# Leaving 246 doubly stored edges to their first place, and fetching the last group's 266 rows one by one, in a graph kernel on Trainium2

## What is computed

```python
ef = relu(edge_attr @ We1 + be1) @ We2 + be2
ef = ef * sigmoid(timestamps[:, None] @ Wt + bt)
combined = concatenate([x[src], ef], axis=1)
msg = relu(combined @ Wn1 + bn1) @ Wn2 + bn2
out = segment_sum(msg, dst, num_segments=6250) + x
result = layernorm(x + out)          # eps 1e-5, no scale or shift
```

## Time and profile before

| | |
|---|---|
| median of 3 runs | 1052.55 us (1051.5 to 1053.58) |
| profiled execution | 1052.93 us, of which the span from its first to its last instruction is 1051.1 us |
| PE busy | 851.2 us (81%) |
| DVE busy | 650.9 us (62%) |
| ACT busy | 592.4 us (56%) |
| POOL busy | 781.9 us (74%) |

### The profile page before, as it was taken

The page is one execution under the profiler, slowest core; times in us unless marked ns, Lnnn a source line. Parts: engine busy times, 40 slices in busy tenths (PEclk is TensorE's granted clock), DMA queues, the critical chain, the costliest instruction groups (busy, mean ns, idle before and its releaser), DMA issues.

```text
span 1051.1 us, 19241 instructions
## 1 busy us (share of the span) xinstructions
PE 851.2 (81%) x5031; PEld 616.9 (59%) x5032; DVE 650.9 (62%) x1688; ACT 592.4 (56%) x658; POOL 781.9 (74%) x832
## 2 busy tenths in 40 slices
PE   6899996988788788787787787887887787787884
PEld 6667674666456556465565665564564565564663
DVE  4767774766655666566466566566557566565666
ACT  5576664665465466455555555555555555555542
POOL 7777777777777777777777777777777777777773
PEclk9999999999998999889999999999999999998997
DMA  8964544444544444444545444444444444444321
GB/s 243 288 213 122 144 144 144 126 144 144 144 144 129 140 154 143 124 146 144 144 137 136 139 144 145 124 143 131 137 144 129 140 143 141 128 144 143 83 54 50
DMA packets 80800, 148.69 MB, mean 141 GB/s; under 512 B 20183, under 2 KB 49174, under 8 KB 80678
## 3 DMA queue, kind: packets, MB, share of 16 engines
q1 hardware_dynamic: 51750, 89.86, 27.0%
q0 software_dynamic: 26336, 53.99, 19.3%
q10 hardware_dynamic: 2592, 3.48, 0.9%
HBM read 140.85 MB, written 6.40 MB: 140 GB/s over the span
## 4 chain that ended last, share of the span: by engine, by line
POOL 52%; issue 24%; PE 8%; DMA 7%; DVE 4%; ACT 2%; SPq 1%; ACTq 0%; DVEq 0%; POOLq 0%
POOL gathered L518 52%; DMA gathered<-node_table,src_e 5%; PE psS L804 3%; PE psM L845 2%; DVE h L1124 2%; DMA x_sb<-in_x 1%; PE psH L858 1%; DMA spans_dram<-span_i 1%; ACT h L590 1%; PE psE L870 1%; ACT x_sb L668 0%; DVE onehot L1130 0%; ACT tw L647 0%; ACT staged_own L683 0%; SPq L417 0%
## 5 line engine op out<-in xcount | busy, mean ns | idle before, releaser
L518 POOL DMA_INDIRECT gathered<-node_table,src_e x791 | 749.8, 948 | 242.5 <-issue 236.6
L655 ACT ACTIVATE h<-psH,be_c 128x1024 f32<-128x1024 f32 x104 | 115.9, 1115 | 334.7 <-PE psH L858 334.6
L804 PE MATMUL psS<-onehot,h 128*128 128x128 f32 x1656 | 228.9, 295 | 63.4 <-ACT h L590 60.2
L1124 DVE TENSOR_TENSOR h<-psM,gathered 128x1024 f32<-128x1024 f32 (+1 forms) x104 | 122.6, 1182 | 224.0 <-DMA gathered<-node_table,src_e 177.3
L804 PEld LDWEIGHTS psS<-onehot,h 128*128 128x128 f32 x1656 | 211.7, 206 | 81.7 <-issue 48.0
L647 ACT ACTIVATE tw<-ew,bt_c,wt_c 128x1024 f32<-128x1024 f32 x104 | 236.0, 2270 | 20.0 <-DVE efw L1145 18.6
L870 PE MATMUL psE<-h,we 128*128 128x512 f32 x416 | 214.6, 640 | 0.0
L845 PE MATMUL psM<-wn,efw 128*128 128x128 f32 x1664 | 207.9, 279 | 4.8 <-DVE h L1124 4.8
L1145 DVE SCALAR_TENSOR_TENSOR efw<-psE,be_c,tw 128x1024 f32<-128x1024 f32 x104 | 133.3, 1282 | 114.1 <-PE psE L870 108.3
L845 PEld LDWEIGHTS psM<-wn,efw 128*128 128x128 f32 x1664 | 199.9, 197 | 5.6 <-DVE h L1124 5.6
L858 PE MATMUL psH<-eaT,we 64*128 64x512 f32 x416 | 122.9, 668 | 74.3 <-DMA gathered<-node_table,src_e 66.7
(11 more groups left out here) (112 smaller groups left out, 339.6 us busy)
## 6 DMA issues: line engine op xcount, KB each, us to landing
ew<-in_edge_weight SPq DMA_DIRECT2D x104, 512.0 KB, 4.3
ea<-in_edge_attr SPq DMA_DIRECT2D x104, 256.0 KB
fetched<-node_table SPq DMA_DIRECT2D x1152, 0.5 KB
gathered<-node_table,src_e POOLq DMA_INDIRECT x791, 2.5
x_sb<-in_x SPq DMA_DIRECT2D x6, 512.0 KB, 9.4
out_y<-x_sb ACTq DMA_DIRECT2D x12, 256.0 KB
node_table<-gathered SPq DMA_DIRECT2D x7, 256.0 KB, 5.2
node_table<-h SPq DMA_DIRECT2D x4, 256.0 KB, 4.0
```

The lines of the kernel that those rows point to most:

```text
L518: pool.indirect_dma_start(to, None, rows, bass.IndirectOffsetOnAxis(index, 0)).then_inc(landed, by)
L655: nc.scalar.activation(h1[:, s % 2, :], psH[:, :, :].rearrange("p r e -> p (r e)"), ACT.Relu, bias=be1_c[:, :]).then_inc(h1_ready, 1)
L804: return nc.tensor.matmul(to, h[:, (k - SUM_LAG) % BODY * PAIR + q, t * C:(t + 1) * C], hot, start=(t == 0), stop=(t == TILES - 1))
L1124: return nc.vector.tensor_tensor(to, of, rows, ALU.add)
```

## The change

- The 246 shared edges stay in group 0 and are dropped in group 207. The memset on VectorE (L1051) goes. GpSimd makes a small table `own_edges` at the start (6250 for an edge number below 266, -1 for the others), and VectorE takes the minimum of it and group 207's node numbers in step 0 (`keep_own_edges`). A wait for it stands before the one-hots of pair 103.
- Group 207 now has 512 - 246 = 266 edges of its own. SyncE fetches their rows one by one into a buffer that the first pairs no longer need (`last_rows`, in `raw_own`): `LAST_ROWS`, 13 a step, in steps 81 to 101 (20 steps of 13 and one of 6). GpSimd gathers nothing for group 207.
- `FETCHED` ends at 77: pairs 87 and 97 have all 8 tiles gathered again. So there are 100 x 8 - 7 - 4 = 789 gathers, and 7 x 128 + 266 = 1162 fetched rows.
- In the last pair the groups change roles: group 207 (q = 1) comes first, in one addition, and group 206 (q = 0) last, tile by tile.

```diff
-FETCHED = list(range(17, 98, FETCH_STEPS))
+FETCHED = list(range(17, 78, FETCH_STEPS))
+LAST_FROM = FETCHED[-1] + 4
...
+    LAST_EDGES = GE - SHARED
+    LAST_ROWS = [(t, p) for t in range(TILES) for p in range(-(-(LAST_EDGES - ORDER[t]) // TILES))]
...
+        last_rows = raw_own[:, RAW - RAW_BEFORE - 1, :]
...
-        last_banks = [psS[:, 0:PAIR * W], psM[:, 0, 0:PAIR * W]]
+        last_banks = [psS[:, 0:PAIR * W], psM[:, 1, 0:PAIR * W]]
...
+            def fetch_last(n):
+
+                wanted = LAST_ROWS[max(0, n - LAST_FROM) * FETCH_ROWS:max(0, n - LAST_FROM + 1) * FETCH_ROWS]
+                for t in range(TILES):
+                    parts = [part for of, part in wanted if of == t]
+                    if not parts:
+                        continue
+                    rows = numbers_of(G - 1, t, range(parts[0], parts[-1] + 1))
+                    for part, row in zip(parts, rows):
+                        sp.dma_start(last_rows[part:part + 1, t * C:(t + 1) * C], table[bass.ds(row, 1), :])\
+                            .then_inc(last_rows_in, 16)
...
                 fetch_rows(n)
+                fetch_last(n)
...
+            pool.memset(own_edges[:, :], float(N)).then_inc(own_step, 1)
+            pool.wait_ge(own_step, 1)
+            pool.affine_select(out=own_edges[:, :], in_=own_edges[:, :], compare_op=ALU.is_gt, fill=-1.0,
+                               base=LAST_EDGES, pattern=[[-1, TILES]], channel_multiplier=-TILES).then_inc(own_ready, 1)
...
-                        if p in FETCHED and q * TILES + t == PAIR * TILES - 1:
+                        if (p in FETCHED and q * TILES + t == PAIR * TILES - 1) or p * PAIR + q == G - 1:
                             continue
...
-                            landed = last_gather_in[0 if q == 0 else 1 + t]
+                            landed = last_gather_in[t]
...
-                for q in range(PAIR):
+                for q in reversed(range(PAIR)):
                     for t in range(TILES):
-                        pe.wait_ge(last_h, 1 if q == 0 else 2 + t)
+                        pe.wait_ge(last_h, 1 if q else 2 + t)
...
-                    dve.wait_ge(dst_shifted, 2)
-                    nc.vector.memset(ids_f[0:1, 1, 0, 0:SHARED], -1.0).then_inc(dst_moved, 2)
...
+                    dve.wait_ge(dst_kept, 1)
                     for q in range(PAIR):
                         hot(PAIRS - 1, k + 1, q)
...
-                    dve.wait_ge(last_gather_in[0], 16 * TILES)
-                    make_pre(h[:, at, :], psM[:, 0, :], gathered[:, at, :]).then_inc(last_pre, 1)
+                    dve.wait_ge(last_rows_in, 16 * len(LAST_ROWS))
+                    make_pre(h[:, at + 1, :], psM[:, 1, :], last_rows).then_inc(last_pre, 1)
...
+            def keep_own_edges():
+
+                last_dst = dst_of(G - 1).rearrange("p (b a) -> p b a", a=2)
+                dve.wait_ge(dst_e_ready, 2)
+                dve.wait_ge(own_ready, 1)
+                nc.vector.tensor_tensor(last_dst, last_dst, own_edges[:, :].rearrange("p (a b) -> p b a", a=2), ALU.min)\
+                    .then_inc(dst_kept, 1)
```

More of the change, by code:

```diff
@@ L148, in gnn_kernel @@
         dst_e = sb("dst_e", [P, G, TILES])
+        own_edges = sb("own_edges", [P, TILES])
         dst_more = sb("dst_more", [P, TILES])
@@ L213, in gnn_kernel @@
         placed = sem("placed")
-        last_gather_in = [sem(f"last_gather_in{i}") for i in range(1 + TILES)]
+        last_gather_in = [sem(f"last_gather_in{i}") for i in range(TILES)]
+        last_rows_in = sem("last_rows_in")
         y_out = sem("y_out")
@@ L221, in gnn_kernel @@
             sem(n) for n in ("raw_xT_ps", "raw_xT_ready", "raw_ps", "raw_ready"))
-        src_cast, dst_cast, dst_moved = sem("src_cast"), sem("dst_cast"), sem("dst_moved")
-        dst_shifted = sem("dst_shifted")
+        own_ready, own_step = sem("own_ready"), sem("own_step")
+        src_cast, dst_cast = sem("src_cast"), sem("dst_cast")
+        dst_shifted, dst_kept = sem("dst_shifted"), sem("dst_kept")
         src_ps, dst_ps, src_e_ready, dst_e_ready = (
@@ L472, in _, with numbers_of @@
             load_weights_of(3)
+            def numbers_of(g, t, parts):
+                return nc.values_load_multi_w_load_instructions(
+                    src_rows[g % P:g % P + 1, g // P, :].rearrange("a (p j) -> a j p", j=TILES)
+                    [:, ORDER[t], parts.start:parts.stop], engines=(SP_ENGINE,), min_val=0, max_val=N - 1,
+                    skip_runtime_bounds_check_because="the edge's source node, which the inputs bound")[1]
             def fetch_rows(n):
@@ L482, in fetch_rows @@
                     sp.wait_ge(placed, f - 1)
-                g = FETCHED[f] * PAIR + PAIR - 1
                 parts = range(at * FETCH_ROWS, min((at + 1) * FETCH_ROWS, P))
[L485 to L488, removed]
+                rows = numbers_of(FETCHED[f] * PAIR + PAIR - 1, TILES - 1, parts)
                 for part, row in zip(parts, rows):
@@ L595, in last_step @@
                 act.wait_ge(last_pre, 1)
-                relu(h[:, at, :]).then_inc(last_h, 1)
+                relu(h[:, at + 1, :]).then_inc(last_h, 1)
                 for t in range(TILES):
                     act.wait_ge(last_pre, 2 + t)
-                    relu(h[:, at + 1, t * C:(t + 1) * C]).then_inc(last_h, 1)
+                    relu(h[:, at, t * C:(t + 1) * C]).then_inc(last_h, 1)
             def copy_raw(n):
@@ L827, in step @@
                 if raw and k == 0:
-                    pe.wait_ge(dst_moved, 2)
+                    pe.wait_ge(dst_shifted, 2)
                     pe.wait_ge(table_ready, len(JOBS) - 1)
@@ L1209, in step @@
                     add_raw_bias(0)
+                    keep_own_edges()
                 if live(i, k, MSG_LAG):
@@ L1245, in last_step @@
                     dve.wait_ge(msg_ps, PAIRS)
[L1246 to L1247 removed]
+                    dve.wait_ge(last_rows_in, 16 * len(LAST_ROWS))
+                    make_pre(h[:, at + 1, :], psM[:, 1, :], last_rows).then_inc(last_pre, 1)
                     for t in range(TILES // 2):
[L1249 removed]
+                        pre_tile(at, t)
                 if s == PAIRS + 2:
@@ L1254, in last_step, with add_sums @@
                     for t in range(TILES // 2, TILES):
-                        pre_tile(at + 1, t)
+                        pre_tile(at, t)
                 if s == PAIRS + 3:
-                    for q in range(PAIR):
-                        dve.wait_ge(sum_ps, PAIRS + q)
-                        add_sums(PAIRS - 1, q, last_sums[q])
-            def add_sums(g, q, of):
-                dve.wait_ge(acc_added, g * PAIR + q)
+                    for n, q in enumerate(reversed(range(PAIR))):
+                        dve.wait_ge(sum_ps, PAIRS + n)
+                        add_sums(PAIRS - 1, q, last_sums[q], n)
+            def add_sums(g, q, of, n=None):
+                dve.wait_ge(acc_added, g * PAIR + (q if n is None else n))
                 add_at(sums, last_lows[g][q], of).then_inc(acc_added, 1)
@@ L1266, in pre_tile @@
                 of = slice(t * C, (t + 1) * C)
-                dve.wait_ge(last_gather_in[1 + t], 16)
-                make_pre(h[:, at, of], psM[:, 1, of], gathered[:, at, of]).then_inc(last_pre, 1)
+                dve.wait_ge(last_gather_in[t], 16)
+                make_pre(h[:, at, of], psM[:, 0, of], gathered[:, at, of]).then_inc(last_pre, 1)
+            def keep_own_edges():
[4 more added lines that the diff above has]
+                    .then_inc(dst_kept, 1)
             def add_raw_bias(n):
```

1 line of the change is left out of this document (removed).

## The result

The changed kernel takes 1056.3 us, median of 22 runs (1053.04 to 1059.13), beside 1053.07 us for the kernel before in the same comparison (22 runs). The ratio is 1.0024, 95% interval 1.0015 to 1.0034: 2.5 us slower, with 1.6 to 3.6 us for the interval; the two medians are 3.2 us apart, which lies within it. The forecast was +2.5 us. The experiments bear out which gathers count. They also show a price that the prediction did not see, that of the rows which SyncE fetches late in the kernel. As both kernels fetch about as many of them, it does not show in the difference, as far as the traces tell; no run settles it.

The account below looks back on a forecast made before the run. Bound: GpSimd's gathers at 1.25 us each up to pair 101's last, then VectorE's work. Two added gathers +2.50 us, all else 0: 1052.93 becomes 1055.43, or 1055.05 us as a median; 8-in-10 range 1052.4 to 1056.9.

Parts of the forecast that it names:

- What sets the end: Kernel's end: the last gather of pair 101 sets it; nothing waits for the last twelve or so gathers.
- Two gathers, +2.50: Pairs 87 and 97, ahead of pair 101's last gather: two more gathers at 1.25 us each, +2.50 us.
- I take the whole price: Added gathers in pairs 87 and 97: the queue hides nothing, as GpSimd's non-issue idle is just 5.9 us; +2.50 us.
- Four gathers fewer, 0: Group 207 in the last pair: its four gathers come behind all that matter, so dropping them gains 0 us.
- The fetch, 0: SyncE, steps 81 to 101: group 207's rows arrive in time on a queue off the chain (1%), 0 us.
- Its cover: SyncE's last rows: they land 80 us before the addition that reads them; failure would cost 2.4 us.
- Rival D: Group 207's addition waits for fetched rows because SyncE falls 80 us behind; somewhere above 1055 us, chance 0.02.
- Start, mask, order of the last pair, clock at the end: 0: GpSimd's and VectorE's start, last pair's order, TensorE's final clock: 0 us each; uncovered start 0.8, later clock rise about 1.
- Port lock: Added gathers beside VectorE instructions with two SBUF inputs: up to 0.39 us more each, sum at most 1055.8 us.

Follow-up runs that it names:

- the one in which TensorE took over: Kernel before without the four gathers of the second group of pair 100 (787 gathers, 771 up to pair 101): ratio 0.9970 (0.9958 to 0.9982).

## Why the prediction was right, and where it was not

**What sets the end.** Right, and now shown from both sides: four gathers behind pair 101 are worth nothing (1.0003), four ahead of it 3.2 us, and the distance from pair 101's last gather to the end stays at 36.0 to 36.8 us in every kernel whose end was not edited, except the one in which TensorE took over.

**Two gathers, +2.50.** Direction, place and price are right: in the stretch in which they stand they cost 2.4 us, and there "I take the whole price" held. The kernel with only the two tiles gathered again is just 1.4 us slower (1.0010 to 1.0016), but it has 256 fetched rows fewer, and what it gains by them lies ahead of pair 80.

**Four gathers fewer, 0.** Right. The forecast of the places was right too but for the late start: last gather of the changed kernel at 1033.7 for 1032.5.

**The fetch, 0.** Right only as a difference, and not for the reason given. Its cover held, as the step said: the rows arrive 80 us early. But rows that SyncE fetches from step 81 on are not free. Without them the kernel is 1 to 2 us shorter, and that lies far ahead of the fetch itself. No row of before pointed to that, and SyncE's 1% of the chain, which the step leaned on, was that of one execution. The kernel before has 256 such rows and the changed one 266, so nearly nothing is left of it in the difference, if both kinds cost the same. By pair 80 they do within the spread of the profiles. If the rows of before cost nothing, then the sum came out right because 1.4 us and the fetch's 1 to 2 us happened to fill it; the whole times alone do not rule that out. Rival D, late rows, did not happen.

**Start, mask, order of the last pair, clock at the end: 0.** Right, each by a kernel (1.0000 for the mask; the order and the four gathers together in 1.0003) or by its rows.

**Port lock.** The prediction let a gather cost up to 0.39 us more beside a VectorE instruction with two inputs in SBUF. One gather at the end of the changed kernel lasted 1.44 us, 0.50 more, again beside such an instruction; VectorE's and GpSimd's timeline:

```profile
1023.17 0.68 DVE L1331 SCALAR_TENSOR_TENSOR staged_own<-x_sb,staged_own 128x512 f32<-128x512 f32 x1
```

```profile
1023.24 1.44 POOL L545 DMA_INDIRECT gathered<-node_table,src_e  x1 [0.30 <-issue]
```

By the Trainium skill ("SBUF — State Buffer", "SBUF: two separate sides") that is the exclusive lock on the shared ports, and the trace agrees once more for a gather that starts behind VectorE's instruction; it fell behind pair 101 and cost nothing. The last section measures it over all the profiles.

The forecast has the right sum and, for the gathers, the right term. A forecast of a total is no proof of its terms, though: the price of the late rows stood on both sides, and only kernels that changed it alone brought it to light.

## What to carry to other kernels

Find the last item of a stream that something still waits for, and price additions and removals by the side of it on which they stand; a cut behind that point buys nothing, however long the stream is on the chain. Time each part of a change by itself even where the sum fits, and ask what else the edit that isolates it takes away: here the two gathers could not be added without dropping 256 fetched rows. And where a kernel waits early on for one chain of transfers and products, compare that stretch between the two traces before a difference at the end is explained at the end.

## What the runs showed of the hardware that was not expected

- The lock has a fixed measure, and it works one way. In the 14 profiles 229 gathers of the table last over 1.0 us. Each of them has VectorE in an instruction with two SBUF inputs 0.12 us after its start (nearly always L1296 or L1088 of the kernel before), and each ends 0.81 to 0.83 us after that instruction does; the longest lasts 1.47 us for 0.94. The other way round VectorE hardly waits: where its 128x512 instruction (L1296) starts while a gather runs, it takes 0.68 to 0.72 us in all 120 cases.
- Reading 13 row addresses into SyncE's registers takes 2.96 us in the changed kernel's chain of waits (start, length, what); with 5.63 us for the 13 transfers behind it and 0.8 us for the step's two other ones, a fetch step keeps SyncE busy for some 9.4 us of about 10. It has little room left, although the chain gives it a small share.

```profile
200.85 2.96 SPq L483
```

- One program of 1052 us spreads by 2.6 to 6.9 us between executions on one core. In the 14 profiles two things differ most: GpSimd's wait for `pre` of pair 4 near 85 us (0.7 to 3.6 us too long) and the time of gathers beyond 0.95 us (1.8 to 4.7 us in sum). The pitch of gathers differs too, 1.251 us in three profiles and 1.249 in the rest, which makes 1.0 us over the 545 gathers from pair 11 to pair 80.
- TensorE was granted less than full speed within the start in four profiles, those with the last fetch. In three it had waited 1.2 to 1.8 us for VectorE just before, in the fourth 2.06 us for edge features; but in two other kernels it had waited 1.9 and 2.3 us for VectorE there and kept its 2.4 GHz, so the wait alone does not decide it.
